# First stage of a hybrid block on one core: the state scan moved into its own step, and GpSimd's order of work changed with it

## The reference, cut to what matters

```python
def step(carry, kv):
    p, q, o = carry
    kt, vt = kv
    no = jnp.maximum(o, u + kt)
    A = jnp.exp(o - no)
    Bc = jnp.exp(u + kt - no)
    y = (A * p + Bc * vt) / (A * q + Bc)
    no2 = jnp.maximum(w + o, kt)
    A2 = jnp.exp(w + o - no2)
    B2 = jnp.exp(kt - no2)
    return ((A2 * p + B2 * vt, A2 * q + B2, no2), y)
...
rvk = jnp.einsum('btc,dc->btd', x, W_rvk)
r, v, k = jnp.split(rvk, 3, axis=-1)
y = jax.nn.sigmoid(r) * wkv(time_decay, time_first, k, v)
return jnp.einsum('btc,dc->btd', y, W_out)
```

## Time and profile before

| | us |
|---|---|
| median of 3 runs (3487.74 to 3488.74) | 3488.43 |
| the profiled execution's own time | 3486.4 |
| its span, first to last instruction | 3484.6 |
| busy in the span: PE | 3204.3 (92%) |
| DVE | 3133.7 (90%) |
| ACT | 2609.9 (75%) |
| POOL | 2485.7 (71%) |
| mean granted TensorE clock, of 1 | 0.965 |

### The profile page before, as it was taken

The page is one execution under the profiler, slowest core; times in us unless marked ns, Lnnn a source line. Parts: engine busy times, 40 slices in busy tenths (PEclk is TensorE's granted clock), DMA queues, the critical chain, the costliest instruction groups (busy, mean ns, idle before and its releaser), DMA issues.

```text
span 3484.6 us, 46858 instructions
## 1 busy us (share of the span) xinstructions
PE 3204.3 (92%) x12704; PEld 2325.5 (67%) x12704; DVE 3133.7 (90%) x5676; ACT 2609.9 (75%) x5276; POOL 2485.7 (71%) x1964
## 2 busy tenths in 40 slices
PE   6898989899999999999999999999999999976738
PEld 5666766676777767676767676767677777754525
DVE  7998984699999999999999999999999999999990
ACT  6777773687888887878887887878787878776740
POOL 1444444396969696969696969697979697968680
PEclk9999999999999999999999999999999999988869
DMA  3222223111111111111121112121211120111110
GB/s 115 67 85 83 72 67 116 58 37 38 43 38 43 41 40 41 41 40 46 37 47 34 47 34 52 28 55 26 57 25 55 25 55 25 55 26 36 28 34 6
DMA packets 119381, 165.39 MB, mean 47 GB/s; under 512 B 8544, under 2 KB 84192, under 8 KB 118624
## 3 DMA queue, kind: packets, MB, share of 16 engines
q1 hardware_dynamic: 119136, 162.63, 16.8%
HBM read 128.39 MB, written 25.69 MB: 44 GB/s over the span
## 4 chain that ended last, share of the span: by engine, by line
POOL 48%; issue 21%; DVE 16%; PE 7%; ACT 4%; DMA 3%; DVEq 1%; POOLq 0%; SPq 0%; ACTq 0%
POOL dBu L938 26%; POOL yacc L951 17%; DVE D L1454 5%; DVE U L1403 4%; PE W L1195 3%; DMA BC<-bc_scratch 2%; DVE prod L1475 1%; PE W L1229 1%; POOL NV L314 1%; DVE D L1478 1%; POOL EO L302 1%; DMA bc_scratch<-bcS 1%; POOL MX L287 1%; DVE qX L668 1%; POOL MX L285 1%
## 5 line engine op out<-in xcount | busy, mean ns | idle before, releaser
L938 POOL TENSOR_TENSOR dBu<-U,BC 128x512 f32<-128x512 f32 x1024 | 1308.6, 1291 | 334.0 <-DMA BC<-bc_scratch 330.4
L1454 DVE TENSOR_TENSOR_SCAN D<-D,hc,dBu 128x256 f32<-128x256 f32 x2048 | 1446.5, 750 | 19.5 <-ACT D L1110 19.4
L1195 PE MATMUL W<-nT,wffn 128*128 128x256 f32 x5632 | 1229.4, 381 | 6.9 <-ACT nT L979 6.9
L1195 PEld LDWEIGHTS W<-nT,wffn 128*128 128x128 f32 x5632 | 1061.6, 189 | 181.1 <-issue 13.4
L1110 ACT ACTIVATE D<-delta,A 128x256 f32<-128x256 f32 x2048 | 891.5, 468 | 350.8 <-DVE yacc L1488 329.7
L951 POOL TENSOR_TENSOR yacc<-yacc,prod 128x512 f32<-128x512 f32 x752 | 957.5, 1273 | 165.7 <-DVE prod L1475 161.2
L1229 PE MATMUL W<-wffn,hT 128*128 128x512 f32 (+1 forms) x1408 | 617.5, 594 | 8.3 <-DVE hT L1372 8.3
L1475 DVE TENSOR_TENSOR prod<-D,BC 128x512 f32<-128x512 f32 x752 | 513.8, 683 | 0.1
L1229 PEld LDWEIGHTS W<-wffn,hT 128*128 128x128 f32 (+1 forms) x1408 | 262.8, 190 | 327.1 <-issue 307.8
L1195 PE MATMUL W<-nT,win 128*128 128x256 f32 x2048 | 452.4, 382 | 30.2 <-ACT xext L1027 22.9
L1195 PEld LDWEIGHTS W<-nT,win 128*128 128x128 f32 x2048 | 391.9, 192 | 92.1 <-ACT xext L1027 23.7
(11 more groups left out here) (133 smaller groups left out, 2981.1 us busy)
## 6 DMA issues: line engine op xcount, KB each, us to landing
BC<-bc_scratch SPq DMA_DIRECT2D x256, 256.0 KB, 4.7
XM<-x_scratch SPq DMA_DIRECT2D x29, 512.0 KB, 6.1
X<-x_scratch SPq DMA_DIRECT2D x17, 512.0 KB, 3.6
ix<-idx SPq DMA_DIRECT2D x33, 255.0 KB, 2.9
X<-x SPq DMA_DIRECT2D x16, 512.0 KB, 3.4
XR<-x SPq DMA_DIRECT2D x16, 512.0 KB, 3.4
x_scratch<-XR SPq DMA_DIRECT2D x16, 512.0 KB, 3.6
out<-X SPq DMA_DIRECT2D x16, 512.0 KB, 2.7
```

The lines of the kernel that those rows point to most:

```text
L938: nc.gpsimd.tensor_tensor(dBu[e % 4][:], U[:, 2 * j:2 * j + 2, :], BC[slot][:, 0:1, :].to_broadcast([P, 2, CH]), ALU.mult).then_inc(s_dBu, 1)
L1195: last = T_.matmul(dst, lhsT, rhs, start=(n == 0), stop=(n == len(terms) - 1))
L1454: V.tensor_tensor_scan(D[:, m, :], D[:, m, :], dBu[e % 4][:, m % 2, :], hc[:, n, m:m + 1], ALU.mult, ALU.add).then_inc(s_scan, 1)
```

## The change

`state(c)` moves on DVE from the head of step c+1 to the middle of step c, behind pick 4 of piece B, in all steps but the last, where it stays behind the stage. On POOL the difference is followed by the power, then by new values and complement, then by the output rows of the same chunk. The complement is written in place over `EK`, and the scans read it there. Between the two a product of two columns, `ticp`, is put. New waits go with it: the new values also wait for the scans before, the difference for `BT` of the chunk before, and the outputs for the `yT` before; the wait on `BT` moves behind the complement.

```diff
+            ticp = buf(pa, "ticp", [TT])
...
                 def outputs(c, s):
 
                     pool.wait_ge(a_s, KH * (c + 1))
+                    pool.wait_ge(a_y, c)
                     nc.gpsimd.tensor_tensor(MX[:], vv[s][:], sX[:, :, 0:CH], ALU.subtract).then_inc(a_mix, 1)
...
                         pool.wait_ge(a_o, KH * (c + 1))
+                        pool.wait_ge(a_beta, least(KH * c))
                         nc.gpsimd.tensor_tensor(EO[:], oX[:, :, 0:CH], oX[:, :, 1:CH + 1], ALU.subtract).then_inc(a_do, 1)
 
-                        if not (isinstance(c, int) and c == 0):
-
-                            pool.wait_ge(a_kl, c + 1)
-                            outputs(c - 1, 1 - s)
                         if below(c, NC - 3):
                             root(c + 3)
 
                         pool.wait_ge(a_new, KH * (c + 1))
+                        pool.wait_ge(a_evac, 6 * (c + 1))
+                        pool.wait_ge(a_s, least(KH * c))
+                        nc.gpsimd.tensor_tensor(NV[:], EK[:], vv[s][:], ALU.mult).then_inc(a_nv, 1)
+                        pool.wait_ge(a_nv, c + 1)
+                        nc.gpsimd.tensor_tensor(ticp[:], mhalf[:], mhalf[:], ALU.mult)
+                        nc.gpsimd.tensor_scalar(EK[:], EK[:], -1.0, 1.0, ALU.mult, ALU.add).then_inc(a_old, 1)
                         pool.wait_ge(a_beta, KH * (c + 1))
-                        pool.wait_ge(a_evac, 6 * (c + 1))
-                        nc.gpsimd.tensor_tensor(NV[:], EK[:], vv[s][:], ALU.mult).then_inc(a_nv, 1)
-                        nc.gpsimd.tensor_scalar(EO[:], EK[:], -1.0, 1.0, ALU.mult, ALU.add).then_inc(a_old, 1)
+                        outputs(c, s)
                         if not below(c, NC - 2) and front:
                             opening_root()
 
                 steps_a(step, pool)
-                outputs(NC - 1, 1)
...
                     for m in range(KH):
-                        V.tensor_tensor_scan(sX[:, m, 1:CH + 1], EO[:, m, :], NV[:, m, :], sX[:, m, 0:1], ALU.mult, ALU.add).then_inc(a_s, 1)
+                        V.tensor_tensor_scan(sX[:, m, 1:CH + 1], EK[:, m, :], NV[:, m, :], sX[:, m, 0:1], ALU.mult, ALU.add).then_inc(a_s, 1)
...
                         if not front:
                             opening_stats()
-                        if not (isinstance(c, int) and c == 0):
-                            state(c - 1)
                         if not front:
                             opening_shift()
...
                         if front:
                             bits(B_, 1, 4)
                         if front:
-                            picks(B_, 1, 4)
-                        if front:
-                            picks(B_, 4, 5)
+                            picks(B_, 1, 5)
+                            state(c)
                         if below(c, NC - 2):
                             bits(A2_, 0, 1)
```

## The result

| | before | after |
|---|---|---|
| median of 5 runs, us | 3487.84 (3486.82 to 3488.74) | 3505.36 (3503.11 to 3506.29) |
| ratio to before, 95% interval | | 1.0050 (1.0038 to 1.0062) |
| span of the profiled execution, us | 3484.6 | 3504.0 |

The change makes the kernel 0.50% slower: 17.5 us in the medians, 19.4 us between the two profiled executions. The prediction was 3502.6 us.

A forecast was written before the change was run, and what follows sets the result against it. DVE's order was taken to set the first-stage step; with the change, steady steps +6.3, steps 0, 1 and 13 +4.4, step 14 +1.4 and PE +2.1 gave +14.2 us, 3502.6 us in the median; 8-in-10 range 3480 to 3511 us.

The forecast's parts named there:

- The hold: First-stage steps: DVE's first carry L646 cannot end until POOL's yT has ended, 1.68 us a step.
- S: Start of the four state scans on DVE in a first-stage step, put at 18.72 us after POOL's difference.
- S to the next difference: Rest of the steady step: yT ends 12.10 us after the scans start, then 0.03, 0.36 and 2.76 to the difference.
- yT itself comes late: Rival, first-stage steps: yT waits for PE's product, some +0.5 us a step, 3508 us; chance 0.10 together with dear ticp.
- DVE's idle time: First-stage steps: 1.39 + 0.27 us of DVE waiting for ACT goes, 0.36 comes; the carry is reached at S + 10.17.
- no hold: Rival, first-stage steps: the carries pass yT unhindered, step 32.29 us, kernel 3479 us; chance 0.20.
- Only the oX scan is held: Rival, first-stage steps: the two-input scan waits for yT, the carries do not; 0.34 us less a step, 3498 us; chance 0.10.
- The forecast's own range: Whole kernel: 3496 to 3511 us, from ticp (0 to 0.7 us) and PE (0 to 4.2 us).
- Steps 0, 1 and 13: First-stage steps where ACT is done sooner: 33.59 us each, together +4.4 us.
- Step 14 to the shift: End of the first stage: the opening norm's shift comes 31.24 us after the difference instead of 29.83, +1.4 us.
- PE at the boundary: Entry to the second stage: PE idles over 5 us and then runs partly at its lower clock, +2.1 us.

The follow-up runs named there:

- e1: The changed kernel without the multiplication by the sigmoid gate, the third output instruction writing yT itself in two buffers: 3490.5 us, 1.0017 of the kernel before.
- e3: The changed kernel with yT moved on POOL behind the next step's difference and a wait for the qX scans: 3492.7 us, 1.0022 of the kernel before.
- e2: The changed kernel with the three carries moved on DVE to behind the subtraction into EO of the step before: 3505.1 us, 1.0057 of the kernel before.
- e5: The kernel before without POOL's wait on a_kl, so the output instructions run straight behind the difference: 3585.3 us, 1.0284 of the kernel before.
- v2: The changed kernel with the edits of e3 and e4 together and no other: 3477.0 us, 0.9975 of the kernel before.
- e4: The changed kernel with A2's low bits ahead of the state scans on DVE and ACT's gates and values ahead of the leaves: 3505.1 us, 1.0058 of before.
- v4: v2 with step 14's state scans behind the last picks and the opening power ahead of its last remaining output instruction: 3476.3 us, 0.9972 of the kernel before.

## Why the prediction was right or wrong

**The hold: right.** It was argued from two rows of one other carry, each ending with a POOL instruction, and it is most of the loss: from the first difference to the first feed-forward product before takes 499.7 us, after 518.2, e1 506.4 and e3 507.0, so 11 to 12 of the 18.4 us go with it. It does not decide the sign alone, as the prediction had it: without it the kernel is still slower than before, by some 7 us. The kernel after shows it at L646, e1 and e3 take it away and give back 0.9 us a step, e2 moves it to the scan. The Trainium skill (SBUF — State Buffer, Who interferes with whom) says that the engine which starts second stands still until the first one's instruction is over, also for DVE instructions with two inputs in that memory; L646 (0.29 us free, 1.07 to 1.33 held), the scans of e2 (2.68 to 3.97) and the turns in e5 agree. The same section says that a DVE instruction with at most one input there, outside the two-port modes, does not contend. The predicate copies name two inputs, but `nX`, `nY` and `nZ` lie in PSUM, and they are not held (0.69 us beside yT in e2); neither is the addition out of PSUM in e3 (1.21 us), so the traces agree there too. A predicate copy with both inputs in the on-chip memory was not tried.

**S: right to 0.24 us.** From the difference to S it was 18.96 for 18.72: new values 0.17 later, 2.45 from them to ticp for 2.33, ticp 0.16 for 0.20 (from its start to that of the complement), the rest within 0.01. ACT's sigmoids ended 14.93 us after the difference, as forecast; it is the start of the new values behind them that took 0.22 for 0.05.

**S to the next difference.** S to the first output 2.82 for 2.77, outputs 9.42 for 9.33, end of yT to the scan 0.38 for 0.39, scan to difference 2.76 for 2.76. The sum is 34.34 in this step and 34.36 in the mean, against 33.97. The 0.39 us a step are, in the mean, 0.23 in S, 0.05 to the first output, 0.08 in the outputs and 0.03 from the scan to the difference, all on the same side; over 11 steps it is 4.3 us, practically the whole miss in the sum (18.4 measured for 14.2). The output group is in part the rival "yT itself comes late": in the step shown PE's product waited for `xnT` and then took 8.7 us, so yT waited for it. In steps 4 to 8 yT stood 0.18 to 0.30 us behind the third output instruction, in the others 0.08. That rival had made PE ready at S + 1.4 and priced the lateness at 0.5 us in every step; it was 0.1 to 0.2 in five.

**The mis-sized term: DVE's idle time.** I let the idle time of 1.39 + 0.27 us go, put 0.36 in its place and had DVE at the carry at S + 10.17. It came at S + 11.08. The idle time moved to piece A2 (0.52 + 0.75 us), since A2's leaf on ACT takes the buffer that the last pick of piece B frees, and that pick was pushed back behind the scans. I had said that ACT's leaves have 1 us of room, and looked at piece B alone. On the time of this kernel it had no effect, for the carry was held anyway: the hold was 0.8 us shorter and its end the same. So the number is right here although this term was wrong, because yT's end and not DVE set the step. Where it mattered was the first rival.

**The rival "no hold", 3479 us: wrongly priced.** Its mechanism was made real in e1 and e3: 3490.5 and 3492.7 us, the step 33.46, not 32.29. With DVE at S + 11.08 the step is 18.96 + 11.08 + 0.64 + 2.80 = 33.48, where 2.80 is the mean from the scan to the difference in e1 and e3 (2.76 and 2.84 in turn). Only with the leaves mended too (v2) did the 32.36 appear. By their ratios of 1.0017 and 1.0022 that is 3494 and 3496 us beside the 3487.84 of before: still 0.2% slower, not 0.2% faster, and the low end of the range, taken from this rival, was some 14 us too low.

**"Only the oX scan is held": half right.** The scan is held, as e2 shows, but the carries ahead of it are as well.

**The range.** The forecast's own range was added up wrongly: 3502.6 less 2.8 for ticp and 2.1 for PE is 3497.7, not 3496, and 3502.6 plus 7.0 and 2.1 is 3511.7, not 3511. The measured 3505.4 lies inside either.

**Steps 0, 1 and 13** 33.63, 33.70 and 33.64 for 33.59; the gain on the time before 4.7 for 4.4. **Step 14 to the shift** 31.25 for 31.24; here yT's end and the statistics' last instruction came within 0.02 us of each other (564.31 and 564.33), so either path would have set it. **PE at the boundary** 1.7 for 2.1; product(13) ran warm (7.03) as forecast, and it was the turn of XM and the projections behind the idle time that were slow, from a granted clock of 0.50 on. The same holds for the two rows the term was taken from: the product of 9.23 us had a granted clock of 0.77 in the mean, behind 4.63 us of idle time, the one of 7.13 us had 1.00.

**Open.** The new values start 0.22 us behind ACT's sigmoids in steps 2 to 11, the hardware loop, and 0.08 us behind them in the steps that are written out; why was not tried, and neither was the 1.0 us ahead of the first difference. The granted clock at the boundary is measured; that PE's idle time of 8.65 us brought it down is argued, for no run changed that idle time alone.

## What to carry to other kernels

When work of GpSimd is moved, write down which DVE instruction will start beside each of its instructions: here the same 2.35 us instruction costs 0.9 us a step beside a carry of four elements, and nothing beside predicate copies whose data lie in PSUM, the addition out of PSUM or the statistics; integer bit operations took 0.66 to 0.68 us each beside POOL's work as elsewhere. Ask of an idle time that is to be filled which buffer or engine made it; a step later the same dependence may stand elsewhere. And when two limits lie within a microsecond of each other, try the mends together before either is called worthless: e4 alone changed nothing, and with e3 it was worth 1.1 us a step.

## What was not expected of the hardware

- Contention between the two engines did not stay with one pair of instructions. In e5 three DVE groups of 4.91 us took 12.82, POOL's output of 2.37 took 3.21, and the kernel lost 99 us by the removal of one wait.
- The price does not go by the size of the held instruction but by what is left of the other engine's: a tensor_scalar of four columns took 1.18 and 2.22 us for 0.29 (L646 after and in e4), a scalar_tensor_tensor of two columns 2.12 for 0.16 (the shift in v4), and a subtraction of 1024 columns 3.18 for 1.23 (e5).
- It works in both directions: POOL's power on two columns, 0.71 before in the median, took 1.61 after (the longest before was 1.60). It starts at 339.74, DVE's lX (L677) started at 339.57 and ended at 340.79, and the power ended 0.56 us later.
